# Unchecked row gathers with in-range padding indices, and the mixers' reciprocal square roots on VectorE

## The chip, the cores and the metric

One NeuronCore of a Trainium2 chip runs the whole program in one launch. The metric is device time in microseconds. The engines are named as the profile names them: PE (TensorE, with PEld for its weight loads), DVE (VectorE), ACT (ScalarE), POOL (GpSimd) and SP (SyncE, which only issues transfers here).

## The reference, cut to what matters

The program computes two stages of a graph network on 6250 nodes of 256 features and 100,000 edges, everything in fp32. What the change touches are the edge sums, done five times (four layers of the first graph network and one of the second), and two kinds of layer norm that are computed beside them:

```python
# first graph network, 4 layers
h = jnp.einsum('ni,rio->rno', X, W)                 # 4 tables of transformed rows
msg = h[etype, src] * inv_deg[:, None]              # one 256-wide row per edge
agg = jax.ops.segment_sum(msg, dst, num_segments=X.shape[0])
...
# second graph network, 1 layer: 8 tables, no inverse degree
msg = all_h[src, rel]
agg = jax.ops.segment_sum(msg, dst, num_segments=h.shape[0])
# mixers (row work that runs behind the edge sums)
x1 = layer_norm(t + x, ln1_g, ln1_b)                # mixer 0, over 256
...layer_norm(y + x1, ln2_g, ln2_b)                 # mixer 0, over 256
k = _layer_norm(k, ln_k_g, ln_k_b)                  # mixer 1, over 64, 4 heads
v = _layer_norm(v, ln_v_g, ln_v_b)                  # mixer 1, over 64, 4 heads
```

with `layer_norm = (x - mean) * rsqrt(var + 1e-5) * g + b`.

## The kernel before

Nodes lie in 49 tiles of 128 rows; three resident tensors hold them all in SBUF. Edges come sorted by destination. `edge_tables` cuts them into at most 832 steps of 128 slots so that a step's edges all go to one tile of 128 destinations; the last step of a tile is padded, and the steps after the last tile are padding alone. For every slot it makes a row number for the gather (`plane` 0 for the four tables, `plane` 1 for the eight), a local destination 0 to 127 (−1 for padding), and a weight. A padding slot's row number is 2^20, past the end of every table.

An edge stage (`EdgeSum`) does the 832 steps as 52 bodies of 16 steps; `s` is a step's place in its body. POOL issues one indirect DMA per step (line 451), which gathers 128 rows of 1 KB from the table in HBM into slot `s` of `msg`, and which drops the rows that fail the bounds check. DVE builds a 128x128 one-hot matrix from the local destinations (lines 462, 464), so that a padding slot's row of it is zero. PE multiplies it with the gathered rows (line 496) into one of four PSUM banks, and DVE adds the bank to the tile's sums (line 482). POOL may take a half body's 8 gathers only once ACT has copied their row numbers (lines 442, 443), which ACT does when PE is through the same half of the body before.

Behind the first three stages of the first network runs one tile of mixer work per body (`Keys0`, `Attend`, `Feed`), hung into the engines' orders by the `after(s)` callbacks, for bodies 0 to 49; `Keys1` runs behind the stage of the second network. The fourth stage has nothing behind it. `Attend`, `Feed` and `Keys1` need a reciprocal root per row: DVE makes mean and variance late in a body (`end_first` at s = 11 or 9, line 1754 at s = 13) and adds eps (lines 655, 1756); POOL raises it to the power −0.5 between two gathers, after s = 4 of the next body (lines 661, 1729); DVE turns it into a shift after s = 5 (lines 667, 1745); ACT normalises with scale and shift (lines 677, 1665).

Every engine has its own program order, written out by hand with semaphores; nothing is reordered.

Of the kernel before, what the change touches and what calls it, by code (L numbers as in the profile page):

```python
# [5 lines left out]
ALU = mybir.AluOpType  # L6
# [7 lines left out]
P = 128  # L14
# [107 lines left out]
def rstd(pool, c, g, s_mv, s_rs, s_tmp):  # L122

    pool.wait_ge(s_mv, (g + 1) * GT)
    c.nc.gpsimd.tensor_tensor(c.ve[:], c.mv[:, :, 1], c.eps7[:], ALU.add).then_inc(s_tmp, 1)  # L125
    pool.wait_ge(s_tmp, g + 1)
    c.nc.gpsimd.tensor_tensor(c.rs[:], c.ve[:], c.pow7[:], ALU.pow).then_inc(s_rs, 1)  # L127

# [59 lines left out]
def edge_tables(nc, c, src, dst, et4, et8):  # L188
# [3 lines left out]
    with Phase(nc, "edges") as ph:  # L192
# [49 lines left out]
        with nc.Block() as block:  # L242
# [33 lines left out]
            def _(dve):  # L276
# [141 lines left out]
class EdgeSum:  # L418
# [26 lines left out]
    def gpsimd(self, pool, n, after=None):  # L445
        for h in range(2):
            pool.wait_ge(self.ring_ready, n * 4 + (2 * h + 2))
            gate(pool, self.c)
            for u in range(HALF):
# [3 lines left out]
                    in_offset=bass.IndirectOffsetOnAxis(ap=self.row_ring[:, h, u:u + 1], axis=0),  # L453
                    bounds_check=self.table.shape[0] - 1, oob_is_err=False).then_inc(self.landed[s], 16)
# [175 lines left out]
class RowsBehind:  # L630
# [4 lines left out]
    def __init__(self, nc, c, ph, name, ex):  # L635
# [3 lines left out]
        self.bn, self.mv, self.ve, self.rs, self.shift = (cut(n) for n in (6, 2, 1, 1, 1))  # L639
        (self.s_in, self.s_turned, self.s_xt, self.s_mm, self.s_act, self.s_mm2, self.s_t, self.s_u, self.s_bn, self.s_mv,  # L640
         self.s_ve, self.s_pow, self.s_rs, self.s_hat, self.s_gam, self.s_bet, self.s_done, self.s_dma) = (
            ph.sem(f"{name}_{n}") for n in (
                "weights_in", "turned", "xt", "first_products", "first_results", "second_products", "rows_begun", "rows_made",
                "partial", "variance", "variance_eps", "powers", "rstd", "normal", "gamma", "beta", "done", "dma"))

    def end_first(self, dve, i):
# [17 lines left out]
    def shift_mean(self, dve, i):  # L664

        dve.wait_ge(self.s_pow, i)
        self.nc.vector.scalar_tensor_tensor(self.shift, self.mv[:, 0:1], -1.0, self.rs, ALU.mult, ALU.mult).then_inc(self.s_rs, 1)
# [26 lines left out]
class Attend(RowsBehind):  # L694
# [84 lines left out]
    def vector(self, dve, i, first, second):  # L779
        v, c = self.nc.vector, self.c  # L780

        def after(s):
            if s == 5 and second:
                self.shift_mean(dve, i)
# [27 lines left out]
class Feed(RowsBehind):  # L812
# [72 lines left out]
    def vector(self, dve, i, first, second):  # L885
        v, c = self.nc.vector, self.c

        def after(s):
            if s == 5 and second:
                self.shift_mean(dve, i)  # L890
# [748 lines left out]
class Keys1:  # L1639
# [6 lines left out]
    def __init__(self, nc, c, ph, wt):  # L1646
# [5 lines left out]
        self.ve, self.rs, self.shift, self.power = (ph.sb(n, [P, NH]) for n in ("kv_ve", "kv_rs", "kv_shift", "kv_power"))  # L1652
        self.zero = ph.sb("zero", [P, D + KH])
        (self.s_set, self.s_x, self.s_turned, self.s_xt, self.s_kv, self.s_bn, self.s_mv, self.s_ve, self.s_rs, self.s_hat,
         self.s_sum, self.s_pow) = ph.sems("kv_set tile_staged tile_turned tile_xt keys_made keys_partial keys_variance keys_variance_eps keys_rstd "
# [20 lines left out]
    def begin_tensor(self, pe):  # L1676
# [4 lines left out]
        pe.wait_ge(self.s_set, 2)  # L1681
# [43 lines left out]
    def gpsimd(self, pool, i, second):  # L1725
        def after(s):
            if s == 4 and second:
                pool.wait_ge(self.s_ve, i)
                self.nc.gpsimd.tensor_tensor(self.rs[:], self.ve[:], self.power[:], ALU.pow).then_inc(self.s_pow, 1)
        return after  # L1730

    def begin_vector(self, dve):
        v = self.nc.vector
        dve.sem_inc(self.s_hat, 1)
        v.memset(self.power[:], -0.5).then_inc(self.s_set, 1)
        v.memset(self.zero[:], 0.0).then_inc(self.s_set, 1)

    def vector(self, dve, i, first, second):
# [3 lines left out]
        def after(s):  # L1742
            if s == 5 and second:
                dve.wait_ge(self.s_pow, i)
                v.scalar_tensor_tensor(self.shift[:], self.mv[:, :, 0], -1.0, self.rs[:], ALU.mult, ALU.mult)\  # L1745
                    .then_inc(self.s_rs, 1)
# [661 lines left out]
```

## Time and profile before

| | |
|---|---|
| median of three runs | 9214.34 us (9209.06 to 9225.05) |
| the profiled execution's own time | 9212.07 us |
| its span | 9210.3 us |
| PE, DVE, ACT, POOL busy | 6617.7, 4380.4, 1368.6, 4814.7 us |

An edge stage takes about 1.09 to 1.17 ms and there are five; the rest is making tables, norms and the two feed-forward parts. A busy PE is not a PE at its peak: the ends of matmuls are modelled. "issue" as the cause of an idle stretch means that the engine waited for nothing that the profile shows. In rows of instructions a duration is followed, in brackets, by the engine's idle time before it.

### The profile page before, as it was taken

Reading aid. Unit: us, or ns where it says so; the run is one execution under the profiler, and the core shown is the slowest. Engines: PE = TensorE matmul, PEld = TensorE weight load, DVE = VectorE, ACT = ScalarE, POOL = GpSimd, SP = SyncE. Lnnn points to the kernel's source line nnn. Section 1 sums busy time; section 2 is a strip of 40 time slices with the busy share of each in tenths; the row PEclk is TensorE's granted clock in tenths of the full one; section 3 lists DMA queues with packets and bytes.
Section 4 is the critical chain, followed back from the end, with each engine's and each line's share of the span. In section 5 each row is a group of like instructions: output and inputs, shape, how many; then the busy total and the mean of one; then the engine's idle time right before and its main releaser. Section 6 shows DMA issues by size and latency. Waiting matters only on the chain. (4 is left out here: it accounts for less than half of the span.)

```text
span 9210.3 us, 102377 instructions
## 1 busy us (share of the span) xinstructions
PE 6617.7 (72%) x18072; PEld 3621.6 (39%) x18072; DVE 4380.4 (48%) x13067; ACT 1368.6 (15%) x3463; POOL 4814.7 (52%) x4543
## 2 busy tenths in 40 slices
PE   0777777587777587777678988818759777775378
PEld 0344433343444244344333333305534444443355
DVE  6135555426666516666533555552243455552512
ACT  0311110221111131111031000002112111110122
POOL 0057777337777517777724777730000677773311
PEclk9887787787777697777686555559879777776789
DMA  1243333133333123333223333300024333330000
GB/s 63 83 132 100 96 96 87 63 106 109 106 105 106 55 98 103 102 100 99 73 74 103 99 96 96 90 10 0 0 68 139 104 91 89 89 89 16 1 20 20
DMA packets 424515, 732.12 MB, mean 79 GB/s; under 512 B 92896, under 2 KB 296939, under 8 KB 424193
## 3 DMA queue, kind: packets, MB, share of 16 engines
q0 software_dynamic: 200240, 514.23, 19.4%
q1 hardware_dynamic: 224206, 217.15, 7.0%
q8 instruction: 21, 0.34, 0.0%
q14 instruction: 48, 0.39, 0.0%
HBM read 587.30 MB, written 176.90 MB: 83 GB/s over the span
## 5 line engine op out<-in xcount | busy, mean ns | idle before, releaser
L451 POOL DMA_INDIRECT gnn_msg<-tables,gnn_row_ring x4160 | 4180.6, 1005 | 1942.0 <-issue 1786.7
L496 PE MATMUL bank<-gnn_msg,gnn_hot 128*128 128x256 f32 x8320 | 3823.4, 565 | 1236.4 <-DMA gnn_msg<-tables,gnn_row_ring 719.3
L496 PEld LDWEIGHTS bank<-gnn_msg,gnn_hot 128*128 128x128 f32 x8320 | 1760.1, 257 | 3138.0 <-DVE gnn_hot L462 1269.7
L482 DVE TENSOR_TENSOR sums<-sums,bank 128x256 f32 x4160 | 1750.8, 421 | 2327.8 <-PE bank L496 2238.5
L462 DVE TENSOR_SCALAR gnn_hot<-iota,gnn_meta_ring 128x128 f32<-128x128 f32 x3328 | 1107.5, 360 | 595.3 <-ACT gnn_meta_ring L443 595.3
L125 POOL TENSOR_TENSOR ve<-mv,eps 128x7 f32<-128x7 f32 x63 | 12.8, 203 | 1796.7 <-DVE mv L119 1648.6
L1004 PE MATMUL bank<-gnn_w,gnn_hot 128*128 128x512 f32 (+1 forms) x2352 | 902.9, 542 | 0.0
L1004 PEld LDWEIGHTS bank<-gnn_w,gnn_hot 128*128 128x128 f32 x2352 | 443.8, 195 | 445.0 <-issue 396.6
L442 ACT COPY gnn_row_ring<-row 128x8 int32 (+1 forms) x520 | 104.3, 201 | 3320.7 <-PE bank L496 3300.0
L990 PE MATMUL bank<-ident,gnn_msg 128*128 128x128 f32 x392 | 64.5, 314 | 405.6 <-ACT gnn_msg L1049 243.7
L1568 PE MATMUL bank<-tables_w,sums 128*128 128x512 f32 x784 | 340.3, 596 | 6.4 <-ACTq L109 6.4
L1066 ACT COPY gnn_msg<-bank 128x512 f32<-128x512 f32 x392 | 229.8, 586 | 510.1 <-PE bank L1004 510.1
L97 PE MATMUL bank<-ident,sums 128*128 128x128 f32 x294 | 49.6, 337 | 332.0 <-DVE sums L135 265.1
L464 DVE TENSOR_SCALAR gnn_hot<-iota,gnn_meta_ring 128x128 f32<-128x128 f32 x832 | 232.7, 305 | 0.3
L1568 PEld LDWEIGHTS bank<-tables_w,sums 128*128 128x128 f32 x784 | 149.2, 191 | 193.6 <-issue 193.6
L990 PEld LDWEIGHTS bank<-ident,gnn_msg 128*128 128x128 f32 x392 | 50.3, 161 | 427.2 <-issue 427.2
L1188 DVE TENSOR_TENSOR sums<-sums,gnn_vecs 128x1792 f32 x28 | 146.6, 5235 | 117.4 <-POOL sums L1153 117.4
L1288 PE MATMUL bank<-sums,ffn_w 128*128 128x512 f32 (+1 forms) x448 | 176.1, 555 | 4.8 <-ACTq L109 4.8
L97 PEld LDWEIGHTS bank<-ident,sums 128*128 128x128 f32 x294 | 43.8, 176 | 342.4 <-issue 342.4
L1581 DVE COPY sums<-bank 128x512 f32<-128x512 f32 x98 | 67.8, 691 | 231.0 <-PE bank L1568 226.9
L1665 ACT ACTIVATE gnn_hat<-bank,gnn_kv_shift,gnn_kv_rs 128x64 f32<-128x64 f32 x392 | 121.4, 415 | 378.5 <-DVE gnn_kv_shift L1745 378.5
L1288 PE MATMUL bank<-sums,experts_w 128*128 128x512 f32 (+1 forms) x448 | 172.8, 547 | 6.4 <-ACTq L109 6.4
(363 smaller groups left out, 5619.6 us busy)
## 6 DMA issues: line engine op xcount, KB each, us to landing
tables<-gnn_msg SPq DMA_DIRECT2D x392, 256.0 KB, 2.1
gnn_msg<-tables,gnn_row_ring POOLq DMA_INDIRECT x4160, 2.8
tables<-sums SPq DMA_DIRECT2D x98, 512.0 KB, 2.9
first_norm<-state SPq DMA_DIRECT2D x1, 6272.0 KB, 27.6
gnn_w<-first_norm SPq DMA_DIRECT2D x49, 128.0 KB
mixer_rows<-gnn_ex SPq DMA_DIRECT2D x49, 128.0 KB, 1.8
gnn_w<-mixer_rows SPq DMA_DIRECT2D x49, 128.0 KB
residual<-in_x_dram SPq DMA_DIRECT2D x1, 6144.0 KB
```

Source lines behind the costliest of these rows:

```text
L451: self.nc.gpsimd.indirect_dma_start(out=self.msg[:, s, :], out_offset=None, in_=self.table, in_offset=bass.IndirectOffsetOnAxis(ap=self.ro ...
L462: ins = self.nc.vector.tensor_scalar(self.hot[:, s, :], self.c.iota[:], m[:, 0:1], m[:, 1:2], ALU.is_equal, ALU.mult)
L464: ins = self.nc.vector.tensor_scalar(self.hot[:, s, :], self.c.iota[:], m[:, 0:1], None, ALU.is_equal)
L482: self.nc.vector.tensor_tensor(at, at, self.c.bank[4 + s % 4][:, 0:D], ALU.add).then_inc(self.added, 1)
L496: self.nc.tensor.matmul(self.c.bank[4 + s % 4][:, 0:D], self.hot[:, s, :], self.msg[:, s, :], start=True, stop=True).then_inc(self.summed, 1)
L990: ins = nc.tensor.transpose(c.bank[b][:, (k - k0) * P:(k - k0 + 1) * P], stage[:, (k - k0) * D + h * P:(k - k0) * D + (h + 1) * P], c.iden ...
L1004: ins = nc.tensor.matmul(c.bank[b][:, 0:width], xt[:, h, k * P:(k + 1) * P], w[:, h, j * 512:j * 512 + width], start=(h == 0), stop=(h == ...
L1066: nc.scalar.copy(outs[:, o, :], c.bank[b][:]).then_inc(s_out, 1)
L1188: v.tensor_tensor(x, x, vecs[:, 2:3, :].to_broadcast([P, GT, D]), ALU.add).then_inc(s_bet, 1)
L1288: ins = nc.tensor.matmul(c.bank[b][:, 0:w * P], self.w1[:, h, m * P:(m + 1) * P], self.xt[:, h, k0 * P:(k0 + w) * P], start=(h == 0), stop ...
L1568: ins = nc.tensor.matmul(c.bank[b][:], xt[:, h, k * P:(k + 1) * P], w[:, h, j * 512:(j + 1) * 512], start=(h == 0), stop=(h == KH - 1))
L1665: self.nc.scalar.activation(self.hat[:, n, :], self.c.bank[1][:, n * self.HD:(n + 1) * self.HD], ACT.Identity, bias=self.shift[:, n:n + 1] ...
```

## The change

- The gather of an edge stage loses its bounds check.
- A padding slot's row number becomes its slot number (0 to 127) in place of 2^20, so that the gather reads a real row there; its one-hot row stays zero. For this, in each of the 7 blocks of `edge_tables` and for each of `plane` 0 and 1, one addition of a constant becomes a subtraction of the tensor `slot_no`, and another an addition of it.
- The power on POOL in `Attend`, `Feed` and `Keys1` goes. `inverse_root`, 13 operations on DVE with a semaphore wait before nearly each, takes its place straight after the variance, and the shift follows it there, in place of its own turn after s = 5 of the next body.
- In the stage of the second network POOL's clearing of `msg` and DVE's memset of the powers go.

```diff
+def inverse_root(dve, c, y, half, t, var, s_step, i):
+    v = c.nc.vector
+    first = i * ROOT_STEPS                                   # ROOT_STEPS = 13
+    v.tensor_scalar(y, var, EPS, None, ALU.add).then_inc(s_step, 1)
+    v.tensor_scalar(half, var, EPS, -0.5, ALU.add, ALU.mult).then_inc(s_step, 1)
+    dve.wait_ge(s_step, first + 2)
+    v.tensor_scalar(t.bitcast(I32), y.bitcast(I32), 1, None, ALU.arith_shift_right).then_inc(s_step, 1)
+    dve.wait_ge(s_step, first + 3)
+    v.tensor_scalar(y.bitcast(I32), t.bitcast(I32), -1.0, ROOT_SEED, ALU.mult, ALU.add).then_inc(s_step, 1)
+    for k in range(3):
+        at = first + 4 + 3 * k
+        dve.wait_ge(s_step, at)
+        v.tensor_tensor(t, y, y, ALU.mult).then_inc(s_step, 1)
+        dve.wait_ge(s_step, at + 1)
+        v.tensor_tensor(t, t, half, ALU.mult).then_inc(s_step, 1)
+        dve.wait_ge(s_step, at + 2)
+        v.scalar_tensor_tensor(y, t, 1.5, y, ALU.add, ALU.mult).then_inc(s_step, 1)
+    dve.wait_ge(s_step, first + ROOT_STEPS)
+    gate(dve, c)
...
 for f in (0, 1):
-    then(v.tensor_scalar(plane[:, b, f, :], recs[:, b, :, f], -float(1 << 20), None, ALU.add))
+    then(v.tensor_tensor(plane[:, b, f, :], recs[:, b, :, f], slot_no[:], ALU.subtract))
     then(v.tensor_tensor(plane[:, b, f, :], plane[:, b, f, :], valid[:, b, :], ALU.mult))
-    then(v.tensor_scalar(plane[:, b, f, :], plane[:, b, f, :], float(1 << 20), None, ALU.add))
+    then(v.tensor_tensor(plane[:, b, f, :], plane[:, b, f, :], slot_no[:], ALU.add))
...
 self.nc.gpsimd.indirect_dma_start(
     out=self.msg[:, s, :], out_offset=None, in_=self.table,
-    in_offset=bass.IndirectOffsetOnAxis(ap=self.row_ring[:, h, u:u + 1], axis=0),
-    bounds_check=self.table.shape[0] - 1, oob_is_err=False).then_inc(self.landed[s], 16)
+    in_offset=bass.IndirectOffsetOnAxis(ap=self.row_ring[:, h, u:u + 1], axis=0)).then_inc(self.landed[s], 16)
...
 # end_first of Attend and Feed
-    v.tensor_scalar(self.ve, self.mv[:, 1:2], EPS, None, ALU.add).then_inc(self.s_ve, 1)
+    inverse_root(dve, c, self.rs, self.ve, self.tmp, self.mv[:, 1:2], self.s_pow, i)
+    v.scalar_tensor_tensor(self.shift, self.mv[:, 0:1], -1.0, self.rs, ALU.mult, ALU.mult).then_inc(self.s_rs, 1)
 def gpsimd(self, pool, i, first, second):
-    def after(s):
-        if s == 4 and second:
-            pool.wait_ge(self.s_ve, i)
-            self.nc.gpsimd.tensor_tensor(self.rs, self.ve, self.c.pow7[:, 0:1], ALU.pow).then_inc(self.s_pow, 1)
-    return after
+    return None
...
 # Keys1: the same for 8 columns, at s = 13; its gpsimd() and the shift at s = 5 go
-    nc.gpsimd.memset(msg[:], 0.0).then_inc(s_zero, 1)
-    pool.wait_ge(s_zero, 1)
-    pool.wait_ge(keys.s_set, 2)
+    pool.wait_ge(keys.s_set, 1)
```

## Rows read from the trace of the kernel before

**Rows 1.** The page's first part: each engine's busy time, share and instructions.

```profile
PE 6617.7 (72%) x18072; PEld 3621.6 (39%) x18072; DVE 4380.4 (48%) x13067; ACT 1368.6 (15%) x3463; POOL 4814.7 (52%) x4543
```

**Rows 2.** Busy time by stretch of the span, all engines; stretches inside edge stages.

```profile
core 0: us, PE busy (x) PEld busy (x) DVE busy (x) ACT busy (x) POOL busy (x), PEclk, DMA share, GB/s
700.00:1500.00 800.00, 601.40 (x1612) 318.62 (x1612) 440.57 (x1306) 88.51 (x345) 613.10 (x614) 0.80 0.34 97
1600.00:1620.00 20.00, 15.69 (x32) 6.87 (x32) 10.20 (x29) 0.30 (x2) 15.41 (x16) 0.66 0.03 2
2050.00:3050.00 1000.00, 737.84 (x2120) 408.25 (x2120) 648.01 (x1994) 102.33 (x367) 778.52 (x790) 0.76 0.37 107
5000.00:6000.00 1000.00, 893.88 (x1534) 379.11 (x1534) 522.48 (x1535) 28.97 (x190) 766.46 (x767) 0.52 0.33 95
7300.00:8250.00 950.00, 743.31 (x2019) 440.50 (x2018) 497.75 (x2106) 157.78 (x589) 749.02 (x715) 0.71 0.31 90
```

**Rows 3.** Line 451's own view: durations as minimum, median and maximum ns.

```profile
L451 POOLq MOVE  x4160: 29/29/38, 535.8 to 8338.7; - x199
L451 POOL DMA_INDIRECT gnn_msg<-tables,gnn_row_ring x4160: 994/998/1259, 536.7 to 8351.8; - x199
```

**Rows 4.** Timeline of POOL, edge tables: the second and last of seven gathers (L271).

```profile
155.06 0.95 POOL L271 DMA_INDIRECT state<-edge_records,edges_e_i  x1 [0.30 <-issue]
...
161.31 0.95 POOL L271 DMA_INDIRECT state<-edge_records,edges_e_i  x1 [0.30 <-issue]
```

**Rows 5.** Timeline of POOL in the second stage, one body and a later gather.

```profile
2511.09 0.99 POOL L451 DMA_INDIRECT gnn_msg<-tables,gnn_row_ring  x1 [0.31 <-issue]
...
2516.30 1.00 POOL L451 DMA_INDIRECT gnn_msg<-tables,gnn_row_ring  x1 [0.31 <-issue]
2517.33 0.58 POOL L661 TENSOR_TENSOR gnn_ex<-gnn_ex,pow 128x1 f32<-128x1 f32 x1
2518.08 1.04 POOL L451 DMA_INDIRECT gnn_msg<-tables,gnn_row_ring  x1 [0.17 <-issue]
...
2531.16 1.19 POOL L451 DMA_INDIRECT gnn_msg<-tables,gnn_row_ring  x1 [0.30 <-issue]
```

**Rows 6.** Timeline of POOL in the fifth stage.

```profile
7503.45 1.00 POOL L451 DMA_INDIRECT gnn_msg<-tables,gnn_row_ring  x1 [0.30 <-issue]
7504.47 1.67 POOL L1729 TENSOR_TENSOR gnn_kv_rs<-gnn_kv_ve,gnn_kv_power 128x8 f32<-128x8 f32 x1
7506.33 1.07 POOL L451 DMA_INDIRECT gnn_msg<-tables,gnn_row_ring  x1 [0.18 <-issue]
...
7520.81 1.01 POOL L451 DMA_INDIRECT gnn_msg<-tables,gnn_row_ring  x1 [0.30 <-issue]
```

**Rows 7.** Timeline of ACT: a ring copy of the second stage, one of the fifth.

```profile
2503.43 0.20 ACT L443 COPY gnn_meta_ring<-meta 128x16 f32 x1
...
7514.12 0.25 ACT L443 COPY gnn_meta_ring<-meta 128x16 f32 x1
```

**Rows 8.** Timeline of DVE in the second stage: work after s = 11, two bodies.

```profile
2508.89 0.42 DVE L482 TENSOR_TENSOR sums<-sums,bank 128x256 f32 x1 [1.29 <-PE bank L496]
...
2509.48 0.16 DVE L797 TENSOR_SCALAR gnn_w<-bank 128x8 f32<-128x8 f32 x1
2509.68 0.20 DVE L799 RECIPROCAL gnn_w<-gnn_w 128x8 f32<-128x8 f32 x1
...
2512.05 0.42 DVE L482 TENSOR_TENSOR sums<-sums,bank 128x256 f32 x1
...
2531.06 0.42 DVE L807 TENSOR_TENSOR gnn_ex<-gnn_ex,gnn_w 128x256 f32<-128x256 f32 x1
```

**Rows 9.** Timeline of DVE in the fourth stage: two additions in a row.

```profile
5501.29 0.42 DVE L482 TENSOR_TENSOR sums<-sums,bank 128x256 f32 x1 [1.00 <-PE bank L496]
...
5502.16 0.42 DVE L482 TENSOR_TENSOR sums<-sums,bank 128x256 f32 x1 [0.19 <-PE bank L496]
```

**Rows 10.** Views of lines 375 and 376 in the edge tables.

```profile
L375 DVE TENSOR_TENSOR sums<-sums x14: 291/293/293, 169.9 to 188.3; 128x128 f32<-128x128 f32 x14
...
L376 DVE TENSOR_SCALAR sums<-sums x14: 226/226/228, 170.2 to 188.7; 128x128 f32<-128x128 f32 x14
```

More of the change, by code:

```diff
@@ L638, in __init__ @@
         self.u = cut(D)
-        self.bn, self.mv, self.ve, self.rs, self.shift = (cut(n) for n in (6, 2, 1, 1, 1))
+        self.bn, self.mv, self.ve, self.rs, self.tmp, self.shift = (cut(n) for n in (6, 2, 1, 1, 1, 1))
         (self.s_in, self.s_turned, self.s_xt, self.s_mm, self.s_act, self.s_mm2, self.s_t, self.s_u, self.s_bn, self.s_mv,
-         self.s_ve, self.s_pow, self.s_rs, self.s_hat, self.s_gam, self.s_bet, self.s_done, self.s_dma) = (
+         self.s_pow, self.s_rs, self.s_hat, self.s_gam, self.s_bet, self.s_done, self.s_dma) = (
             ph.sem(f"{name}_{n}") for n in (
                 "weights_in", "turned", "xt", "first_products", "first_results", "second_products", "rows_begun", "rows_made",
-                "partial", "variance", "variance_eps", "powers", "rstd", "normal", "gamma", "beta", "done", "dma"))
+ "partial", "variance", "powers", "rstd", "normal", "gamma", "beta", "done", "dma"))
     def end_first(self, dve, i):
@@ L1651, in __init__ @@
         self.bn, self.mv = ph.sb("kv_bn", [P, NH, 6]), ph.sb("kv_mv", [P, NH, 2])
-        self.ve, self.rs, self.shift, self.power = (ph.sb(n, [P, NH]) for n in ("kv_ve", "kv_rs", "kv_shift", "kv_power"))
+        self.ve, self.rs, self.tmp, self.shift = (ph.sb(n, [P, NH]) for n in ("kv_ve", "kv_rs", "kv_tmp", "kv_shift"))
         self.zero = ph.sb("zero", [P, D + KH])
-        (self.s_set, self.s_x, self.s_turned, self.s_xt, self.s_kv, self.s_bn, self.s_mv, self.s_ve, self.s_rs, self.s_hat,
-         self.s_sum, self.s_pow) = ph.sems("kv_set tile_staged tile_turned tile_xt keys_made keys_partial keys_variance keys_variance_eps keys_rstd "
+        (self.s_set, self.s_x, self.s_turned, self.s_xt, self.s_kv, self.s_bn, self.s_mv, self.s_rs, self.s_hat,
+         self.s_sum, self.s_pow) = ph.sems("kv_set tile_staged tile_turned tile_xt keys_made keys_partial keys_variance keys_rstd "
                                "keys_normal keys_summed powers")
@@ L1723, in tensor @@
         return after
[L1725 to L1730, printed above, removed]
     def begin_vector(self, dve):
@@ L1742, in after @@
         def after(s):
[L1743 to L1746, printed above, removed]
             if s == 13 and first:
@@ L1755, in after @@
                 dve.wait_ge(self.s_mv, (i + 1) * NH)
-                v.tensor_scalar(self.ve[:], self.mv[:, :, 1], EPS, None, ALU.add).then_inc(self.s_ve, 1)
+                inverse_root(dve, c, self.rs[:], self.ve[:], self.tmp[:], self.mv[:, :, 1], self.s_pow, i)
+                v.scalar_tensor_tensor(self.shift[:], self.mv[:, :, 0], -1.0, self.rs[:], ALU.mult, ALU.mult)\
+                    .then_inc(self.s_rs, 1)
         return after
@@ L1797, in _ @@
             def _(pool):
-                nc.gpsimd.memset(msg[:], 0.0).then_inc(s_zero, 1)
-                pool.wait_ge(s_zero, 1)
-                pool.wait_ge(keys.s_set, 2)
+                pool.wait_ge(keys.s_set, 1)
                 gate(pool, c)
-                bodies(pool, lambda i, first, second: edges.gpsimd(pool, i + n0, keys.gpsimd(pool, i, second)))
+                bodies(pool, lambda i, first, second: edges.gpsimd(pool, i + n0))
             @block.vector
```

14 lines of the change are left out of this document (4 added, 10 removed).

## The prediction

> **What bounds the kernel now.** I read the page's busy shares first. No engine is full: PE 72%, POOL 52%, DVE 48% [rows 1]. An average over stages says little here, so next I cut the span into stretches [rows 2]. What to see is the length of a stretch over POOL's count in it. Where POOL has gathers alone, 1000 us for 767 is 1.304 us each (fourth stage) and 800 us for 614 is 1.303 (first). With one power per 16 gathers it is 1.344 in the second stage (1000 us for 744, the count of 790 less 46 powers) and 1.41 in the fifth (950 us for 673, 715 less 42). The step is the same at a granted clock of 0.80 and of 0.52, so PE is not what sets it.
>
> The line's own view says what a gather costs POOL: 998 ns at the median, 994 at the least, over all 4160 [rows 3]. The timeline adds 0.30 us before each next gather, put down to "issue" and not to a semaphore [rows 5]. 1.00 + 0.30 is the step of the stage. POOL works without a pause for anybody: the five stages' 4160 gathers, 4160 × 1.30 = 5.4 ms of the 9.2, are a chain on POOL alone. A power stands in that chain too: the gather after it starts 1.78 us after the one before (2516.30 to 2518.08) [rows 5], in the fifth stage 2.88 us (7503.45 to 7506.33) [rows 6].
>
> How near is the next bound? POOL may start a half body once ACT has copied its row numbers. The copy for the gather at 2511.09 began at 2503.43 and took 0.20, so it was there 7.5 us early [rows 5, 7]; in the fifth stage the copy of 7514.12 (0.25 us) was 6.4 us ahead of the gather at 7520.81 [rows 6, 7]. That is five gathers of slack between POOL and everything behind it. So a nanosecond off POOL's step is a nanosecond off the stage, and DVE work costs nothing as long as it holds PE up by less than about 6 us.
>
> **Gathers without the check.** The trace holds seven gathers that have no bounds check, in the edge tables, on the same engine with 128 indices each and 2 KB rows. From the second to the last start, 155.06 to 161.31, five steps take 6.25 us: 1.25 each, of which 0.95 is the gather and 0.30 the same issue gap [rows 4]. The checked ones have a register move of 29 ns besides [rows 3], but the gap is 0.30 with it and without it, so the move is hidden and worth nothing. The check costs 1.30 − 1.25 = 0.05 us. It is a price on another shape, with rows of twice the size; since a checked gather whose slots are nearly all padding (1600 to 1620, DMA share 0.03) keeps POOL busy for 15.41 of 20 us, the same 0.77 as 766.46 of 1000 [rows 2], I read the price as one of 128 indices and not of bytes. 4160 × 0.051 (998 less 947) = **−212 us**. Bounds: none of it, if the difference is the shape's; above, a little more than it, since nothing excludes that a 1 KB row is cheaper than a 2 KB one: another 0.01 would be 42 us.
>
> **Padding that reads real rows.** 832 × 128 − 100,000 = 6,496 rows more per stage, 6.5% more traffic on DMA engines that are busy 0.37 of the time at most [rows 2]. They don't limit anything. The wholly padded gathers at a stage's end now land rows too; I bound that by a gather's own length, 1.0 us for each of the five tails, below by nothing, and take 1 in all.
>
> **Powers off POOL.** `Attend` and `Feed` have 49 each. Without the power the next gather starts 1.30 after the last in place of 1.78, and it is itself 1.04 in place of 1.00: 98 × (0.48 + 0.04) = **−51 us**. `Keys1` has 49: 49 × (2.88 − 1.30 + 0.07) = **−81 us** [rows 5, 6].
>
> **Newton steps on DVE.** 13 operations on 128x1 or 128x8 and the shift come where one add stood. The nearest small dependent pair starts 0.20 apart, wait included (2509.48 to 2509.68) [rows 8], so 13 × 0.20 = 2.6 us more in a row at s = 11, 9 or 13, and one shift fewer after s = 5. None of it counts as long as it is covered. What stands behind it on DVE is the next addition. Today the pause between the additions of s = 11 and 12 is 3.16 us (2508.89 to 2512.05) [rows 8]; it becomes 5.8. PE has four banks, so it goes on for four steps, 4 × 1.25 = 5.0 us, and then stands for about 1 us. POOL has 6.4 us or more in hand, so it never sees this. It is caught up in a few steps: two additions follow PE 0.87 us apart even in the stage at clock 0.52 [rows 9], against 1.25 between gathers. DVE's load per body stays below the body: 648.0 us busy of 1000 is 0.648 × 16 × 1.344 = 13.9 us a body, plus 2.6, of 20.0 [rows 2]. If the cover were gone the steps would cost 147 × 2.6 = 382 us; if each dependent op took 0.3 in place of 0.2, the pause would be 7.1 us and PE would stand 2.1, still inside the slack. ACT gets its scale and shift earlier than before, so its normalisation only moves away from the ring copies.
>
> **Against it.** DVE work can also slow the gathers themselves. One gather took 1.19 in place of 1.00, begun at 2531.16 beside DVE's addition of two SBUF operands from 2531.06 [rows 5, 8]: 0.19 lost. The mean of the fourth stage, where a one-hot runs beside nearly each gather, is 766.46 / 767 = 0.999 [rows 2], so the 128x128 one-hots do no harm. Ten of the new operations read two tensors. If one gather in ten bodies were hit for 0.19 it is 3 us; if every body were, 28. The second and fifth stages show means of (778.52 − 46 × 0.58) / 744 = 1.010 and (749.02 − 42 × 1.67) / 673 = 1.009 [rows 2, 5, 6]. The powers' aftermath is 0.04 to 0.07 in 16 of it, counted above; the other 0.006 to 0.008 has no cause that I can see and may go with the powers or stay with DVE's work (nothing to −20 us over 2496 gathers). I take the two against each other as nothing.
>
> The Trainium skill, page "SBUF — State Buffer", section "SBUF: two separate sides", says that GpSimd and DVE share a port pair as an exclusive lock, held for the whole instruction, against DVE operations in a two-port mode, and against those with two SBUF inputs where GpSimd reads SBUF. By that rule every new step could hold up descriptor making for its own duration, and the sum would lose up to the tenfold of the small bound. By that rule, the trace agrees for the one gather at 1.19, and disagrees for the one-hots, beside which gathers stay at 1.00; so the rows decide, and it stays a rival.
>
> **Edge tables and starts.** 28 operations of 128x128 become two-tensor ones: 293 in place of 226 ns, 28 × 0.067 = +2 us at most, once [rows 10]. POOL's clearing and the memset at the fifth stage's start lie beside the loading of the row numbers: nothing.
>
> **The sum.** −212 − 51 − 81 + 2 + 1 = −341. Against the profiled execution's own 9212.1 (span 9210.3, so 1.8 lie around it; the median of the runs is 2.2 above it) that is 8871; I say **8870 us**, 3.7% less.
>
> **Rivals.**
> 1. *The price of the unchecked gather doesn't carry over.* The 51 ns belong to the table of edge records. Only the powers go: 9212 − 132 + 3 = 9083. For it: another shape. Against: seven equal gathers, and a checked gather whose price doesn't depend on what it moves. Chance 0.10.
> 2. *The new steps hold up gathers.* If the ten two-input steps of 0.15 us each cost POOL their own length in all 147 bodies, 147 × 1.5 = 220 back: 9090; a third of it, 8945. For it: the one gather at 1.19. Against: the one-hots. Chance 0.07, mostly near the third.
> 3. *A stage with work behind it becomes bound by the loop of PE, DVE and ACT.* Its body then keeps more than 20.0 us; halfway between 20.0 and the 20.8 of a stage without powers is 147 × 0.4 = 59 us back: 8930. For it: PE busy 0.74 to 0.89 of a stage. Against: the slack of 6.4 us. Chance 0.07.
> 4. *Slower: DVE becomes the bound in three stages.* The place is the Newton chain, with its integer steps, which the trace shows on no such tile. DVE has 20.0 − 13.9 = 6.1 us a body free. To be slower than before, 147 bodies must lose the 341 us, 2.3 us each beyond that: the chain must take 6.1 + 2.3 = 8.4 us, 0.65 an operation in place of 0.20. At 0.67 it takes 8.7, and the time is 8871 + 147 × 2.6 = 9253. Against: the small operations in view take 0.16 and 0.20. Chance 0.04.
> 5. *Cheaper than the edge-table gather*, by 0.01 or so: 8830. Chance 0.05.
>
> The forecast has 0.67, with its own range 8845 to 8900.
>
> **How the numbers follow.** A measurement of this kernel tells about 0.2% from no change, 18 us. Rivals 1, 2, 3 and 5 and the forecast are all faster by over that: 0.10 + 0.07 + 0.07 + 0.05 + 0.67 = 0.96. Of rival 4, 0.03 is slower and 0.01 is for the stretch between 0.63 and 0.66 an operation, where loss and gain meet. The range leaves out rival 1 and rival 4 and the bad half of rival 2, some 0.17 (0.10 + 0.04 + 0.03): 8820 to 8980.
>
> **What the profile will show.** L451's median near 947 ns with 0.30 before it and no move. Starts 1.25 apart in all five stages, and no power between s = 4 and 5, so that the five stages have nearly the same length, about 1040 us. DVE's pause at s = 11 near 5.8 us, PE waiting for line 482 more often there, and ACT's copies still 5 us or more ahead. The prediction is wrong if the median stays at 998 (rival 1), if its mean stands well over its median (rival 2), or if POOL's idle time is put down to ACT's copies (rivals 3 and 4).

## The result and the profile after

The changed kernel takes 8869.7 us (median of 4 runs) against 9215.9, a ratio of 0.962 [0.960, 0.964]: 346 us less, where 341 were forecast. Two more batches gave 8871.7 against 9214.6, 0.963 [0.961, 0.964], and 8873.0 against 9214.2, 0.963 [0.961, 0.965]. One of the first four runs took 10,960 us; the ratio leaves it out, and it has no trace. The profiled execution took 8865.25 us, its span is 8863.5.

The first part of its page, and three of its costliest groups (answers to [rows 1]):

```profile
PE 6322.2 (71%) x18072; PEld 3511.4 (40%) x18072; DVE 4665.9 (53%) x14830; ACT 1360.0 (15%) x3463; POOL 4442.4 (50%) x4395
...
L477 POOL DMA_INDIRECT gnn_msg<-tables,gnn_row_ring x4160 | 3951.4, 950 | 2045.0 <-issue 1791.0
L521 PE MATMUL bank<-gnn_msg,gnn_hot 128*128 128x256 f32 x8320 | 3600.9, 541 | 1185.2 <-DMA gnn_msg<-tables,gnn_row_ring 701.1
...
L507 DVE TENSOR_TENSOR sums<-sums,bank 128x256 f32 x4160 | 1745.2, 420 | 1613.6 <-PE bank L521 1489.9
```

POOL's busy time fell by 372 us and its instructions by 148: the 147 powers and one clearing. DVE's busy time rose by 286 us, with 1763 instructions more, and the program is shorter all the same. The gathers' mean (950) stands 4 ns over their median (946, below), 16 us over all of them; the prediction had put such lengthened gathers at nothing.

Busy time by stretch, about the first, second, fourth and fifth stage (answers to [rows 2]):

```profile
core 0: us, PE busy (x) PEld busy (x) DVE busy (x) ACT busy (x) POOL busy (x), PEclk, DMA share, GB/s
700.00:1500.00 800.00, 589.80 (x1678) 313.10 (x1678) 467.94 (x1358) 92.41 (x360) 605.34 (x640) 0.86 0.36 105
2050.00:3000.00 950.00, 679.79 (x2094) 408.35 (x2092) 715.85 (x2513) 93.47 (x355) 715.49 (x745) 0.78 0.40 116
4800.00:5700.00 900.00, 809.81 (x1439) 344.24 (x1440) 493.87 (x1438) 27.33 (x180) 680.99 (x720) 0.55 0.36 105
6900.00:7800.00 900.00, 696.02 (x2117) 403.07 (x2115) 598.04 (x2584) 169.41 (x601) 633.38 (x669) 0.82 0.37 107
```

Length over POOL's count: 800/640 = 1.250 us in the first stage and 900/720 = 1.250 in the fourth. The other two stretches reach beyond their stages (the second stage's last gather starts at 2984.6, the fifth's first at 6963.1), so their quotients say nothing; from the table below the second stage's step is 1048.7/831 = 1.262. The step is again the same at a granted clock of 0.86 and of 0.55: PE is still not what sets it.

The view of the gathers' line (durations as minimum, median, maximum; answers to [rows 3]):

```profile
L477 POOL DMA_INDIRECT gnn_msg<-tables,gnn_row_ring x4160: 942/946/1321, 540.4 to 8003.3; - x199
its engine sat idle before it (us, times) until:
  issue: 1791.0, 4084
  ACT gnn_meta_ring L469: 254.0, 76
```

946 ns where it was 998, and no move before it. Of the 254.0 us of wait for ACT's copies, 231.4 are two waits ahead of a stage (144.7 and 86.7).

POOL in the second stage, its gathers from s = 0 of a body on, while DVE is still at s = 11 of the body before (answers to [rows 5]):

```profile
2420.65 0.95 POOL L477 DMA_INDIRECT gnn_msg<-tables,gnn_row_ring  x1 [0.30 <-issue]
2421.90 0.95 POOL L477 DMA_INDIRECT gnn_msg<-tables,gnn_row_ring  x1 [0.30 <-issue]
2423.15 0.94 POOL L477 DMA_INDIRECT gnn_msg<-tables,gnn_row_ring  x1 [0.30 <-issue]
...
2430.68 0.95 POOL L477 DMA_INDIRECT gnn_msg<-tables,gnn_row_ring  x1 [0.30 <-issue]
```

And DVE at the same time, around the Newton chain (answers to [rows 8]):

```profile
2418.30 0.42 DVE L507 TENSOR_TENSOR sums<-sums,bank 128x256 f32 x1 [0.41 <-PE bank L521]
...
2421.28 0.15 DVE L138 TENSOR_SCALAR gnn_ex<-gnn_ex 128x1 f32<-128x1 f32 x1
...
2421.71 0.15 DVE L143 TENSOR_SCALAR gnn_ex<-gnn_ex 128x1 int32<-128x1 int32 x1
2421.90 0.19 DVE L147 TENSOR_TENSOR gnn_ex<-gnn_ex 128x1 f32<-128x1 f32 x1
2422.13 0.16 DVE L149 TENSOR_TENSOR gnn_ex<-gnn_ex 128x1 f32<-128x1 f32 x1
...
2423.48 0.16 DVE L151 SCALAR_TENSOR_TENSOR gnn_ex<-gnn_ex 128x1 f32<-128x1 f32 x1
2423.80 0.16 DVE L681 SCALAR_TENSOR_TENSOR gnn_ex<-gnn_ex 128x1 f32<-128x1 f32 x1 [0.15 <-DVE gnn_ex L151]
2424.11 0.42 DVE L507 TENSOR_TENSOR sums<-sums,bank 128x256 f32 x1
2424.75 0.42 DVE L507 TENSOR_TENSOR sums<-sums,bank 128x256 f32 x1
```

The chain of 13 runs from 2421.28 to 2423.64, 2.4 us. The pause in the additions is 2418.30 to 2424.11, 5.81 us, and after it they come 0.64 apart until they are level again. PE stands 1.23 us for it, where the prediction had about 1:

```profile
2424.68 2.05 PE L521 MATMUL bank<-gnn_msg,gnn_hot 128*128 128x256 f32 x4 [1.23 <-DVE sums L507]
```

Three gathers run right beside the chain, at 0.94 to 0.95 us each. ACT's copy for the gather at 2430.68 ends at 2423.94 (answers to [rows 7]), 6.7 us early:

```profile
2423.74 0.20 ACT L469 COPY gnn_meta_ring<-meta 128x16 f32 x1
```

From the gathers' records, first to last start of each stage (us) and the median gather in ns:

| stage | before | after | change | median before | median after |
|---|---|---|---|---|---|
| 1 | 1083.6 | 1040.9 | −42.7 | 998 | 946 |
| 2 (`Attend`/`Feed`) | 1116.5 | 1048.7 | −67.8 | 1002 | 946 |
| 3 (`Attend`/`Feed`) | 1113.2 | 1042.2 | −71.0 | 1002 | 946 |
| 4 | 1084.8 | 1040.4 | −44.4 | 998 | 946 |
| 5 (`Keys1`) | 1168.4 | 1040.2 | −128.2 | 1002 | 946 |

Together −354; the rest of the program is 7 us longer (9210.3 − 354 + 7 = 8863.5), half of it ahead of the first gather, which starts at 540.4 where it was 536.7.

### The profile page after: what moved, and what is told of

It is laid out like the page before. It is cut to its first block and busy times, and to the rows that moved or that the text cites. A ratio compares the mean times of both kernels' runs of the same rounds, so it can differ in the third digit from the quotient of the medians.

```text
span 8863.5 us, 101707 instructions
## 1 busy us (share of the span) xinstructions
PE 6322.2 (71%) x18072; PEld 3511.4 (40%) x18072; DVE 4665.9 (53%) x14830; ACT 1360.0 (15%) x3463; POOL 4442.4 (50%) x4395
## 2 busy tenths in 40 slices
DMA packets 424513, 765.22 MB, mean 86 GB/s; under 512 B 84857, under 2 KB 288845, under 8 KB 424194
## 5 line engine op out<-in xcount | busy, mean ns | idle before, releaser
L477 POOL DMA_INDIRECT gnn_msg<-tables,gnn_row_ring x4160 | 3951.4, 950 | 2045.0 <-issue 1791.0
L521 PE MATMUL bank<-gnn_msg,gnn_hot 128*128 128x256 f32 x8320 | 3600.9, 541 | 1185.2 <-DMA gnn_msg<-tables,gnn_row_ring 701.1
L521 PEld LDWEIGHTS bank<-gnn_msg,gnn_hot 128*128 128x128 f32 x8320 | 1717.9, 248 | 2932.9 <-issue 1202.5
L487 DVE TENSOR_SCALAR gnn_hot<-iota,gnn_meta_ring 128x128 f32<-128x128 f32 x3328 | 1139.0, 375 | 594.4 <-ACT gnn_meta_ring L469 594.4
L489 DVE TENSOR_SCALAR gnn_hot<-iota,gnn_meta_ring 128x128 f32<-128x128 f32 x832 | 236.1, 321 | 0.1
```

The source lines that it names most:

```text
L477: self.nc.gpsimd.indirect_dma_start(out=self.msg[:, s, :], out_offset=None, in_=self.table, in_offset=bass.IndirectOffsetOnAxis(ap=self.ro ...
L487: ins = self.nc.vector.tensor_scalar(self.hot[:, s, :], self.c.iota[:], m[:, 0:1], m[:, 1:2], ALU.is_equal, ALU.mult)
L489: ins = self.nc.vector.tensor_scalar(self.hot[:, s, :], self.c.iota[:], m[:, 0:1], None, ALU.is_equal)
L521: self.nc.tensor.matmul(self.c.bank[4 + s % 4][:, 0:D], self.hot[:, s, :], self.msg[:, s, :], start=True, stop=True).then_inc(self.summed, 1)
```

## The experiments

Line 451 of the kernel before is 477 in the changed one and 478 where a line was added; 482 is 507 or 508.

### Each half alone: `gathers_alone`, `roots_alone`, and the whole again: `changed_again`

`gathers_alone` has the gather and the in-range padding, and the powers stay on POOL:

```diff
-                    in_offset=bass.IndirectOffsetOnAxis(ap=self.row_ring[:, h, u:u + 1], axis=0),
-                    bounds_check=self.table.shape[0] - 1, oob_is_err=False).then_inc(self.landed[s], 16)
+                    in_offset=bass.IndirectOffsetOnAxis(ap=self.row_ring[:, h, u:u + 1], axis=0)).then_inc(self.landed[s], 16)
```

`roots_alone` has the rest of the diff: `inverse_root` on DVE, no powers, checked gathers and the padding of before.

> The same kernel as only_gathers (gathers' change alone, powers still on POOL), again, because in the four runs just made VectorE's own sequencer took about 700 ns in place of 40 to 57 for hundreds of register instructions inside the edge stages, in the kernel before too. If VectorE's sequencer is quiet, theory: 9000 to 9006, gather median 946 to 952 ns and no POOL idle time from ACT's copies beyond some us. If the halves only work together: 9030 or more. If the sequencer stalls again, all stages with gathers are set by it and the ratio to before is near 1.

> The same kernel as only_roots, again, for the same reason. Quiet sequencer, theory: 9215 - 51 - 81 = 9083, gather median 998 in all five stages; 9072 to 9083 if the 4 ns excess of stages 2, 3 and 5 was the powers' aftermath. If the Newton steps hold gathers up: 9095 or more. With a stalling sequencer: slower than before, since VectorE gets 12 operations more per body and no slack is left to hide them.

> The changed kernel as it is, beside its halves on one chip. Quiet sequencer: 8865 to 8875, so that the halves' savings (about 213 and 132) add up to the whole. Stalling sequencer: above 10400, no faster than before, because POOL then waits for ACT's copies in every body.

| kernel | us | ratio to before (9214.6) | less | stages (us) |
|---|---|---|---|---|
| gathers_alone | 9004.2 | 0.977 [0.975, 0.978] | 210 | 1041.0, 1073.2, 1069.9, 1040.3, 1126.7 |
| roots_alone | 9064.5 | 0.984 [0.982, 0.985] | 150 | 1083.2, 1084.1, 1082.7, 1084.5, 1084.0 |
| changed_again | 8871.7 | 0.963 [0.961, 0.964] | 343 | 1040.9, 1052.8, 1042.5, 1040.7, 1039.9 |

The gathers' line in the two halves, from the costliest groups of each page:

```profile
L451 POOL DMA_INDIRECT gnn_msg<-tables,gnn_row_ring x4160 | 3965.7, 953 | 1940.2 <-issue 1782.4
```

```profile
L477 POOL DMA_INDIRECT gnn_msg<-tables,gnn_row_ring x4160 | 4156.6, 999 | 1959.6 <-issue 1944.5
```

The first half is worth 210 us and the second 150. In `roots_alone` all five stages have one length, 1084: a stage with a Newton chain in each body is as long as one without, so the chain of 13 is covered wholly while a body lasts 20.8 us. The two halves add to 360 and the whole measures 343, so 17 us are lost where they meet. The runs of before spread over 23 us in this batch, so the times alone don't carry that difference; the traces do. By the stages' lengths 14 us are lost, 12 of them in the second stage and 3 in the third, and the other three come to about nothing together.

### Is it the check or the dropped rows: `checked_in_range`

The changed kernel, its padding on real rows, with the bounds check put back. It tells the check's price from that of the rows that a check drops.

> The changed kernel with the bounds check put back on the gathers; the padding still reads rows 0 to 127. Theory: the bounds check itself is what POOL pays for, whatever the rows are: gather median 998, time 8870 + 212 = 9082, as only_roots. Rival: what was dear is a row that is out of bounds (a dropped row, an empty packet); then the median is near 946 and the time near 8870 although the bounds check is there.

Its gathers' line, with the check on and every row in range:

```profile
L477 POOLq MOVE  x4160: 29/29/38, 538.3 to 9789.9; - x199
L477 POOL DMA_INDIRECT gnn_msg<-tables,gnn_row_ring x4160: 992/998/1327, 539.2 to 9796.0; - x199
```

998 ns, as with padding out of range. The check costs POOL 52 ns a gather whether it drops anything or not. (Its whole time belongs to the batch told below: 10,665.9 us, 1.028 [1.025, 1.032] of before. Only the duration on POOL is read here, and that is the same in all batches.)

### A longer chain: `rounds6_again`

The Newton steps run six rounds in place of three, 22 operations in place of 13; the surplus rounds refine a root that is already there.

```diff
-ROOT_STEPS = 13
+ROUNDS = 6
+ROOT_STEPS = 4 + 3 * ROUNDS
...
-    for k in range(3):
+    for k in range(ROUNDS):
```

> The same kernel as rounds6 (six Newton rounds in place of three, 1.8 us more in a row in 147 bodies), again. Quiet sequencer, theory: covered, 8870 within 0.1%. Rival (VectorE's chain already sets the stages with work behind): 9135, or about 9000 if it is partly covered. Stalling sequencer: slower than changed_again by most of 147 x 1.8 = 265 us.

8907.0 us, 0.966 [0.965, 0.968] of before, 35 more than the changed kernel in the same batch. Nine operations, 0.197 us from start to start, in 147 bodies are 9 × 0.197 × 147 = 261 us; 35 of them show. Stages: 1041.3, 1060.8, 1048.8, 1041.1, 1057.9, which is 8 us more than the changed kernel in the second stage, 6 in the third and 18 in the fifth. The 35 us have two causes.

In the fifth stage the slack is used up. POOL there, from the timeline:

```profile
7531.44 0.95 POOL L478 DMA_INDIRECT gnn_msg<-tables,gnn_row_ring  x1 [0.30 <-issue]
7533.32 0.94 POOL L478 DMA_INDIRECT gnn_msg<-tables,gnn_row_ring  x1 [0.93 <-ACT gnn_meta_ring L470]
```

ACT's copy ends at 7532.51. In 39 of the 52 bodies POOL waits for it, up to 0.6 us longer than its usual gap and 15.8 us together. This is the wait that the prediction named as the sign of rivals 3 and 4, and it is there with nine operations more than the change has.

In the second and third stage POOL waits for nothing, but gathers themselves are longer (by 7.9 and 6.3 us together, against `changed_again`). Two of the second stage:

```profile
2418.64 1.16 POOL L478 DMA_INDIRECT gnn_msg<-tables,gnn_row_ring  x1 [0.30 <-issue]
2420.10 1.21 POOL L478 DMA_INDIRECT gnn_msg<-tables,gnn_row_ring  x1 [0.31 <-issue]
```

```profile
2418.56 0.42 DVE L803 SCALAR_TENSOR_TENSOR gnn_w<-gnn_w 128x256 f32<-128x256 f32 x1
...
2420.07 0.42 DVE L806 TENSOR_TENSOR gnn_ex<-gnn_ex,gnn_w 128x256 f32<-128x256 f32 x1
```

Each of the two gathers began just behind the start of a DVE operation with two tensor operands in SBUF, and took 0.21 and 0.26 us longer than 0.95. Those operations had 0.34 and 0.39 us left at the gathers' starts, 0.13 more than the delay in both. The pairs of a gather and an operation of some lines of the two traces, sorted by when the operation began against the gather's start. Median of the gathers in ns and number of pairs (a gather is 946 alone):

```
DVE began, us against   changed     changed     six rounds   six rounds   Newton steps with
the gather's start      line 802    line 808    line 806     line 823     two tensors, changed
-0.5 to -0.3            946 (7)     946 (12)    946 (1)      -            946 (151)
-0.3 to -0.2            977 (25)    998 (23)    -            -            946 (160)
-0.2 to -0.1            1068 (4)    1081 (5)    1137 (2)     -            946 (97)
-0.1 to 0               1206 (6)    -           1206 (44)    946 (1)      946 (186)
0 to 0.1                1280 (4)    948 (1)     -            946 (32)     946 (97)
0.1 to 0.95             946 (10)    946 (18)    1009 (3)     946 (16)     946 (783)
```

(One operation can stand in two rows, against each of two gathers.) The delay falls by 0.1 us for each 0.1 us that the operation began earlier. The seven traces in which DVE runs freely (this one, before, the changed kernel's three and both halves) agree: 262 times such a 256-wide operation had begun at least 0.05 us before a gather and ran on for 0.18 us or more after the gather's start, and in 261 of them the gather was longer by what was left of the operation, less 0.13 us, within 0.02 us.

For operations that began later, from 0.05 us before to 0.16 us after the gather's start, the outcome differs. In front of 219 of them DVE was idle, and 217 held nothing up, though they ran at the start of the gather too (line 823 above). The other 131 followed another operation without a pause, and 104 of them held the gather to the same rule, most of them line 802 behind a one-hot. The largest delay is 0.445 us, in `changed_third`. What sets these apart is not taken further.

The one-hots hold gathers up as well. In the fourth stage of the changed kernel, with nothing but one-hots and additions on DVE, from the timelines of POOL and DVE:

```profile
5088.35 1.03 POOL L477 DMA_INDIRECT gnn_msg<-tables,gnn_row_ring  x1 [0.30 <-issue]
5087.96 0.60 DVE L487 TENSOR_SCALAR gnn_hot<-iota,gnn_meta_ring 128x128 f32<-128x128 f32 x2
```

The pair of one-hots ends at 5088.56, 0.21 us behind the gather's start, and the gather is 0.08 longer. In the seven traces one-hots that had begun over 0.145 us before a gather and still ran 0.16 us behind its start held it up by the same rule 408 times of 424; of those that began nearer to it, most did not. The additions, whose second operand lies in PSUM, did so 7 times of 1586. Together, of the 1974 gathers in these traces that are over 12 ns longer than their stage's median, the rule with these two kinds of operation covers 1641, and 293 more follow a power.

So what it costs is a matter of phase: the three extra rounds are not themselves what holds the gathers up, they shift other operations onto the gathers' starts. In the changed kernel 23 of the 49 operations of line 802 hold a gather up by over 40 ns, and 2 of line 805; here 44 and 46 of the same two operations (lines 803 and 806). Line 808 goes the other way, from 23 to 1 (line 809).

### A batch in which DVE and PE stand still: `only_gathers`, `only_roots`, `rounds6`

The same kernels as `gathers_alone`, `roots_alone` and `rounds6_again`, run earlier on another chip together with `checked_in_range`.

> The kernel before with the gathers' change alone; the powers stay on POOL between two gathers. If the check's price is POOL's own, as I hold: gather median 946 to 952 ns, stages 1 and 4 about 1041 us long and stages 2, 3 and 5 about 1041 + 26, 1041 + 26 and 1041 + 81; time 9215 - 212 to 218 + 3 = 9000 to 9006. If instead the two halves of the change only work together (the unchecked gather is faster only where no power runs beside it, or a second bound comes in while the powers are still there), the saving is well under 200 us: 9030 or more.

> The kernel before with the roots on VectorE alone; the gathers keep their check and the padding its out-of-range rows. If the powers cost POOL their place in the chain and nothing else: 9215 - 51 - 81 = 9083, gather median 998 in all five stages, and the stages about 1084 us each. If the gathers' excess of 4 ns in stages 2, 3 and 5 before was the powers' aftermath, it is gone and the time is 9072 to 9083. If the Newton steps hold gathers up at a cost to the stage, it is 9095 or more.

> The changed kernel with six Newton rounds in place of three: nine more small dependent operations, 9 x 0.2 = 1.8 us more in a row on VectorE in 147 bodies. Theory: covered. VectorE is busy about 15.1 us plus the gaps of a body of 20.0 and the gathers run 7 us ahead, so the time stays at 8870 (within 0.1%). Rival (VectorE's chain already sets the stages with work behind): plus 147 x 1.8 = 265 us, 9135; half of it if it is only partly covered.

| kernel | us | ratio to before (10,364.7 there) |
|---|---|---|
| only_gathers | 10,468.6 | 1.009 [1.006, 1.012] |
| only_roots | 10,653.2 | 1.026 [1.022, 1.029] |
| checked_in_range | 10,665.9 | 1.028 [1.025, 1.032] |
| rounds6 | 10,817.7 | 1.043 [1.039, 1.046] |

The kernel before took 12% longer there than elsewhere, and neither half gained. The gathers are not to blame, their line in `only_gathers`:

```profile
L451 POOL DMA_INDIRECT gnn_msg<-tables,gnn_row_ring x4160: 940/946/1207, 538.9 to 9595.7; - x199
its engine sat idle before it (us, times) until:
  issue: 1735.4, 3927
  ACT gnn_meta_ring L443: 1268.3, 216
```

POOL waits for ACT's copies 216 times and 1268 us. Behind that wait, DVE and then POOL in the fourth stage, from their timelines:

```profile
6229.63 0.42 DVE L481 TENSOR_TENSOR sums<-sums,bank 128x256 f32 x1 [2.78 <-issue]
...
6240.21 0.42 DVE L481 TENSOR_TENSOR sums<-sums,bank 128x256 f32 x1 [9.64 <-issue]
```

```profile
6242.98 0.95 POOL L451 DMA_INDIRECT gnn_msg<-tables,gnn_row_ring  x1 [0.30 <-issue]
6251.36 1.04 POOL L451 DMA_INDIRECT gnn_msg<-tables,gnn_row_ring  x1 [7.43 <-ACT gnn_meta_ring L443]
```

In the 9.64 us DVE waits for no semaphore. The records of its sequencer show in them six instructions of some 700 ns (a branch has 1.38 us), with gaps as long between most of them; the register instructions among them otherwise take 40 or 57 ns. In this trace 1070 register instructions of DVE took over 500 ns, 772 us together; in `before`, `after`, `gathers_alone`, `roots_alone` and `changed_third` not one did.

They are not the whole of it. By stage they are 12, 154, 380, 524 and 0, yet the first and the fifth stage, too, are 287 and 368 us longer than in `gathers_alone`. There it is PE that stands without a wait that the profile shows:

```profile
885.12 3.78 PE L589 MATMUL bank<-gnn_w 128*128 128x512 f32 x4 [4.66 <-issue]
```

Such stands of PE of over 2.5 us are 58 in the first stage and 46 in the fifth (319 and 254 us); `gathers_alone` has none in the first and one in the fifth. What DVE's and PE's stands have in common stays open.

Either way the banks between PE and DVE fill or run dry, ACT gets its row numbers late, and the 7 us of slack are exceeded: in 207 of the 260 bodies POOL waits over 1 us for ACT's copies. Then POOL no longer sets the end: 52 ns off its step buy nothing, and the chain on DVE counts. That is the case of rival 3, reached by a cause that no row of before shows.

### How the chain counts there: `rounds1`, `rounds9`, `rounds13`

The same edit with ROUNDS 1, 9 and 13. They ran on a third chip, on which the kernel before took 10,379.0 us and DVE and PE stood still again; so they don't show where the cover ends while DVE runs freely, for which they were meant. One round leaves the root coarse.

> The changed kernel with one Newton round in place of three: 7 operations in place of 13, a chain of about 1.4 us. The root is coarser (a relative error near 0.2 per cent), nothing else is left out. My theory: the steps are covered except for two small effects, gathers held up beside DVE work in the second stage (8 us over 1040) and nothing elsewhere. So the first and fourth stages stay at 1041, the third and fifth at 1040 to 1042, and the second comes down from 1048.7 to between 1040 and 1046: 8862 to 8870 in all. If the small steps themselves, by their number, held up gathers or put off PE, 6 of 13 gone would give back about half of the 17 us by which the two halves measured apart exceed the whole: 8855 to 8862. If the interaction has nothing to do with the chain's length, 8871 and a second stage of 1049.

> The changed kernel with nine Newton rounds: 31 operations, 18 more than three rounds have, 3.5 us more a body in three stages. DVE has 20.0 less about 15.6 us free in a body with the three rounds, so the added time still fits into the body's 20.0 us, but the pause of about 9.3 us in DVE's additions goes well past the four steps that PE's banks give, and it eats the 7 us of slack between ACT's copies and POOL's gathers. My theory: with six rounds the cost was 35 us of a possible 265; at nine it is past the knee in the fifth stage, where the copies had come down to 0.8 us ahead, and near it in the others. Stages two and three 1060 to 1110, the fifth 1090 to 1150, 8970 to 9070 in all. If only DVE's load counts and the pause doesn't, nearly all is still covered: under 8930. If each added op is on the path from the first one, 18 x 0.2 x 147 = 529 us over 8871: 9400.

> The changed kernel with thirteen Newton rounds: 43 operations, 30 more than three rounds have, 5.9 us more a body. DVE's load in a body is then about 13.9 + 2.6 + 5.9 = 22.4 us against POOL's 20.0, so DVE bounds the three stages with a chain: 2.4 us a body over 147 bodies are 350 us, plus what was lost already on the way: 9220 to 9320, and POOL's idle time is put down to ACT's copies. The first and fourth stages stay at 1041. If DVE's body has more air than I count (PE's waits overlap its own), the body stays near 21 us: 9020 to 9100. If the chain was fully on the path: 30 x 0.2 x 147 = 882 over 8871, 9750.

| rounds | operations | us | ratio to before | stages 1 to 5 (us) |
|---|---|---|---|---|
| 1 | 7 | 10,480.8 | 1.009 [1.007, 1.012] | 1303, 1382, 1457, 1236, 1454 |
| 9 | 31 | 10,934.9 | 1.053 [1.051, 1.056] | 1301, 1565, 1428, 1237, 1734 |
| 13 | 43 | 11,322.8 | 1.090 [1.087, 1.093] | 1306, 1711, 1553, 1238, 1866 |

The expectations, made for a DVE that runs freely, missed in all three. What follows from the table is the price where nothing covers the chain: from 9 to 13 rounds 388 us for 12 × 147 operations, 0.22 us each, a little over the 0.197 from start to start in the timeline. Stages 1 and 4, which have no chain, keep their length. Between 1 and 9 rounds it is 454 us for 24 × 147, 0.13 each. But DVE's slow register instructions fell from 1146 to 480 between these two traces, and the third stage from 1457 to 1428 us, so this price holds a change of the disturbance too. The first part of the page of `rounds13` shows that no engine is near full even so:

```profile
PE 5770.0 (51%) x18072; PEld 3623.9 (32%) x18072; DVE 5244.6 (46%) x19240; ACT 1361.5 (12%) x3463; POOL 4448.8 (39%) x4395
```

### The changed kernel beside before once more: `changed_third`

It was meant to put the changed kernel itself into such a batch, and came to a fourth chip, on which DVE ran freely.

> The changed kernel, word for word, timed beside the kernel before once more. In two batches the kernel before took 10,365 and 10,379 us, and DVE's sequencer spent some 10 us in every body in a row of register instructions of 700 ns each; one Newton round measured 1.0093 of the kernel before there and six rounds 1.0426. My theory: where that happens POOL waits for ACT's ring copies, so that the gather's 0.05 us buys nothing and the Newton chain counts with its full length, and the changed kernel lies between those two, 1.015 to 1.035 of the kernel before, near 10,600 us. Where it doesn't happen and the kernel before takes 9215, POOL is the bound and the time is 8870 again, 0.963. Rival: the gain on POOL is kept in both cases, since the gathers themselves take 946 ns in both: then 350 us less beside either, 10,020 or 8870.

8873.0 us against 9214.2, 0.963 [0.961, 0.965], the time of the theory for that case. The other case, the changed kernel beside a before of 10,370, wasn't measured. Its neighbours bracket it: one round 1.009, six rounds 1.043, on two chips with the same time of before. So three rounds should be slower than before there, by 1 to 4% (`checked_in_range`, which has them beside checked gathers, is, at 1.028); this is argued from its neighbours and not shown.

## Why the prediction was right

**What bounds the kernel.** Right. In the fourth stage POOL's step was 1.305 (1084.8/831) and is 1.252 (1040.4/831), and every nanosecond came off the stage: 4160 × 0.052 = 216 us, where the five stages of `gathers_alone` are 215 shorter and its whole time 210.

**The price of the check.** Forecast −212 from seven gathers of another shape, measured −210. Rivals 1 and 5 (the price doesn't carry over, or the gather is cheaper still) are out: 946 ns here with 1 KB rows, 0.95 us there with 2 KB. `checked_in_range` shows that the price is that of the check. The move of 29 ns was hidden, as said: the gap is 0.30 with and without it.

**Powers.** Forecast −132, measured −150. The difference is the term that I set to nothing. Most of the 0.006 to 0.008 us by which the means of the second and fifth stage stood over 0.998 and the aftermath went with the powers: in `roots_alone` the median is 998 in all five stages, in `gathers_alone` it stays 6 and 3 and 3 ns over 946 in the stages that have powers. Powers lengthen the gathers of the whole body, not only the next one. In the sum of durations the three stages of before stand 9.8, 6.5 and 7.0 us over the first stage, 23 in all, of which I had counted 98 × 0.04 + 49 × 0.07 = 7; the other 16 explain the 18.

**Newton steps.** Forecast 2.6 us and a pause of 5.8, measured 2.4 and 5.81. The pause reached neither POOL nor the stage: the copies stayed 6.7 us ahead, and `roots_alone` has equal stages. Rival 4 (0.65 us an operation, integer steps dear) is out: they take 0.15 on 128x1, and on 128x8 the shift (line 141) 0.17 and the step behind it (line 143) 0.29 at the median, 0.41 at most. How far the cover reaches is now known from one side: of nine operations more, seven eighths still stay hidden, and the first stage to show a wait is `Keys1`'s.

**Contention with the gathers.** I took it as nothing against the up to 20 us that might leave with the powers. Both were there. In `changed_again` the gathers over their stage's median add up to 14.1 us in the second stage and 3.8 in the third, where `roots_alone` has 2.3 and 0.8. These 15 us are most of the 17 between the halves' sum and the whole; the edge tables' cost (14 × 0.106 + 14 × 0.067 = 2.4 us by the operations' durations) stands in `gathers_alone` too and is no part of it. Two steps were wrong in the choice of the culprit. Rival 2 charged the ten two-input Newton steps, and they cost nothing: beside them gathers take 946 ns in every phase. At 0.16 us on 128x1 they are also too short to begin 0.05 us before a gather and run on for 0.13 us after its start. And the prediction cleared the one-hots by a mean of 0.999, which hides single gathers: in the fourth stage of before, one-hots hold up 58 of 832, by 2.2 us together. In the second stage of `changed_again` 9.5 us are held by the 256-wide operations of `Attend`, which stood in the kernel before too, and 4.1 by one-hots; in `roots_alone` it is 1.4 and 0.4. The one gather at 1.19 that the prediction shows fits the rule: line 807 ends 0.32 us after its start, and 0.32 less 0.13 is the 0.19 lost.

The Trainium skill, page "SBUF — State Buffer", section "SBUF: two separate sides", says that whichever of a DVE operation with two SBUF inputs and a GpSimd instruction that reads SBUF starts first has the shared port pair until it ends, and the other is blocked. By that rule, the trace agrees for a 256-wide operation that began at least 0.05 us before the gather: the gather is longer by what is left of the operation, less 0.13 us. It agrees too for additions with their second operand in PSUM, beside which the median stays 946. The same section of the Trainium skill puts DVE operations in a two-port mode under the rule too; whether the one-hots, which do hold gathers up, run in one no run shows. The prediction's word that the trace disagrees for the one-hots was wrong either way, since it rested on their mean.

**The sum.** −341 forecast, −346, −343 and −341 measured. It is nearer than its terms deserve: −18 and +17 were left out, and that they cancel is luck.

## What to carry to other kernels

Where one engine issues a chain of equal instructions and everything behind it has slack, take the step from the length of a stage over its count, look for the price of a change per step in another instruction of the same engine in the trace (here it carried over from rows of 2 KB to rows of 1 KB, which a run had to show), and measure the slack of the next engine in microseconds: it says how much work may be moved there for nothing (here 13 operations of 0.2 us against 6.4 us), and how little of a disturbance of that engine turns the gain around. When work is taken off an engine, look also at what its removal does to the instructions after it, not only to the next. And when gathers on GpSimd show a mean over their median, look for VectorE operations that run at the gathers' starts, those with two SBUF tensors first; whether moving them by a fraction of a step gives the time back was not tried here.

## What the runs showed of the hardware that I had not expected

- A gather of 128 indices takes POOL 946 ns unchecked with 1 KB rows (0.95 us with 2 KB) and 998 checked, with padding rows in range or out of it. Rows out of range don't lower the packet count: packets are 424,515 before and 424,513 after, while the bytes rose from 732 to 765 MB. But before had 8040 packets of 16 bytes, 11 ns each at the median, where the changed kernel has ones of 4 KB, 159 ns each.
- A gather is held up by a 256-wide two-tensor SBUF operation of DVE that began at least 0.05 us before it and still runs 0.13 us after its start, until the operation's end (261 of 262 pairs), and by one-hots that began over 0.145 us before it (408 of 424).
- Powers on POOL add 3 to 6 ns to the median gather of their stage (952, 949 and 949 in `gathers_alone`, 946 without them), besides 0.04 to 0.07 us to the next one.
- On two of the four chips of the experiments the kernel before took 10,365 and 10,379 us in place of 9215. The traces from there have 480 to 1146 register instructions of DVE of some 700 ns, and 127 to 312 places where PE stands for over 2.5 us without a wait that the profile shows; the others have none and one. The DMA traffic for instructions was the same (45 to 48 packets on that queue with and without it), and POOL's gathers kept their 946 ns. What stretches these instructions stays open: no run took it apart.
